# A GRU and a transformer block on one core: queries and keys of six heads instead of four made beside the recurrence, output and feed-forward weights split later

## What is computed

```python
def cell(h, x):                      # 128 steps, one after the other
    gi, gh = x @ W_ih + b_ih, h @ W_hh + b_hh
    r, z = sigmoid(i_r + h_r), sigmoid(i_z + h_z)
    n = tanh(i_n + r * h_n)
    return (1.0 - z) * n + z * h
x = x + gru(x)                       # B, T, D = 16, 128, 256
x1 = ln(x) * (1 + scale1) + shift1   # scale, shift, gate from the condition
q, k, v = x1 @ qkv_w + qkv_b         # H = 16 heads of DH = 128
a = softmax(q @ k.T * DH ** -0.5) @ v
x2 = x + gate1 * (a @ out_w + out_b)
y = gelu((ln(x2) * (1 + scale2) + shift2) @ ffn_w1 + ffn_b1) @ ffn_w2 + ffn_b2
out = x + x2 + gate2 * y
```

## Time and profile before

| | before |
|---|---|
| median of 3 runs (lowest to highest) | 746.58 us (746.04 to 747.35) |
| the profiled execution's own time | 746.35 us |
| its span, first to last instruction | 744.5 us |
| TensorE busy | 711.3 us (96%) |
| VectorE busy | 580.8 us (78%) |
| ScalarE busy | 484.9 us (65%) |
| GpSimd busy | 104.4 us (14%) |
| chain that ended last | TensorE 83%, VectorE 6%, ScalarE 4%, DMA 3%, issue 2% |

### The profile page before, as it was taken

The page is one execution under the profiler, slowest core; times in us unless marked ns, Lnnn a source line. Parts: engine busy times, 40 slices in busy tenths (PEclk is TensorE's granted clock), DMA queues, the critical chain, the costliest instruction groups (busy, mean ns, idle before and its releaser), DMA issues.

```text
span 744.5 us, 25735 instructions
## 1 busy us (share of the span) xinstructions
PE 711.3 (96%) x10644; PEld 525.3 (71%) x10644; DVE 580.8 (78%) x1625; ACT 484.9 (65%) x1665; POOL 104.4 (14%) x134
## 2 busy tenths in 40 slices
PE   6789999999999989999999999999999999999997
PEld 5688888888888767767667677676666767644555
DVE  5778888888888877777788888788887888834643
ACT  4455666556555666767787777776778776675453
POOL 0232222322322200000000101010110101000040
PEclk9999999999999999999999999999999999999999
DMA  6311121111211012222322222222232233300001
GB/s 237 100 48 46 47 83 51 46 45 46 88 38 40 3 30 43 44 37 49 46 44 44 43 45 44 43 44 49 40 50 43 45 52 37 47 19 29 29 6 52
DMA packets 77869, 36.74 MB, mean 49 GB/s; under 512 B 70540, under 2 KB 73784, under 8 KB 77752
## 3 DMA queue, kind: packets, MB, share of 16 engines
q1 hardware_dynamic: 77175, 33.52, 20.4%
q10 hardware_dynamic: 576, 1.57, 0.6%
HBM read 16.20 MB, written 2.10 MB: 25 GB/s over the span
## 4 chain that ended last, share of the span: by engine, by line
PE 83%; DVE 6%; ACT 4%; DMA 3%; issue 2%; SPq 1%; POOL 0%; DVEq 0%; POOLq 0%
PE bank L429 21%; PE bank L431 20%; PE bank L430 20%; PE bank L536 12%; PE bank L544 5%; DVE h_hi L1211 3%; DMA pT_lo<-p_lo 3%; PE bank L449 2%; ACT zg L937 2%; DVE nu L1205 1%; SPq L308 1%; PE bank L436 1%; DMA x<-in_x 1%; PE bank L458 0%; PE bank L478 0%
## 5 line engine op out<-in xcount | busy, mean ns | idle before, releaser
L431 PE MATMUL bank<-y_lo,w_hi 128*128 128x512 f16 (+2 forms) x496 | 139.8, 300 | 0.0
L429 PE MATMUL bank<-y_hi,w_hi 128*128 128x512 f16 (+2 forms) x496 | 139.7, 300 | 0.1
L430 PE MATMUL bank<-y_hi,w_lo 128*128 128x512 f16 (+2 forms) x496 | 139.8, 300 | 0.0
L536 PE MATMUL bank<-h_hi,whh_hi 128*128 128x16 f16 x1536 | 111.1, 177 | 17.6 <-DVE h_hi L1211 15.2
L536 PEld LDWEIGHTS bank<-h_hi,whh_hi 128*128 128x128 f16 x1536 | 88.8, 96 | 36.7 <-DVE h_hi L1211 34.1
L536 PE MATMUL bank<-h_hi,whh_lo 128*128 128x16 f16 x1536 | 109.5, 176 | 0.4 <-issue 0.4
L997 ACT ACTIVATE prob<-bank,nmx 128x128 f32<-128x128 f32 x256 | 90.4, 366 | 29.8 <-DVE nmx L1286 29.8
L536 PEld LDWEIGHTS bank<-h_hi,whh_lo 128*128 128x128 f16 x1536 | 89.4, 96 | 0.6 <-issue 0.5
L429 PE MATMUL bank<-w_hi,y_hi 128*128 128x128 f16 x512 | 89.1, 219 | 0.5 <-DVE v_lo L1290 0.5
L431 PE MATMUL bank<-w_lo,y_hi 128*128 128x128 f16 x512 | 89.1, 219 | 0.0
L430 PE MATMUL bank<-w_hi,y_lo 128*128 128x128 f16 x512 | 89.1, 219 | 0.0
(11 more groups left out here) (156 smaller groups left out, 2132.9 us busy)
## 6 DMA issues: line engine op xcount, KB each, us to landing
stage<-in_weights SPq DMA_DIRECT2D x16, 640.0 KB, 4.1
x<-in_x SPq DMA_DIRECT2D x16, 128.0 KB, 4.0
out<-xr SPq DMA_DIRECT2D x3, 512.0 KB, 3.1
xr<-in_ada_r SPq DMA_DIRECT2D x1, 1024.0 KB, 7.4
pT_hi<-p_hi SPq DMA_TRANSPOSE x64, 2.4
pT_lo<-p_lo SPq DMA_TRANSPOSE x64, 2.5
xr<-in_W_ih ACTq DMA_DIRECT2D x2, 384.0 KB, 3.9
xr<-in_W_hh ACTq DMA_DIRECT2D x2, 384.0 KB, 5.2
```

The source lines that it names most:

```text
L429: mm(ps, w[0], a[0], start=start, stop=False, skip_group_check=True)
L430: mm(ps, w[1], a[0], start=False, stop=False, skip_group_check=True)
L431: return mm(ps, w[0], a[1], start=False, stop=stop, skip_group_check=True)
L536: nc.tensor.matmul(out(m0 + m), half[:, k, (m0 + m) * P:(m0 + m + 1) * P], h_hi[:, k * B:(k + 1) * B, 1], start=False, stop=False, skip_gr ...
```

## The change

1. `AHEAD` is 0, 4, 6, 8, 11, 14. An item is now q or k (one part) of one head for two blocks: 6 matmuls of 256 columns, one high and one low half of 256 columns each. The items run at steps 0, 2, 3, 4, 6, 7 of a block (block 4 also at step 5; block 2 only at step 7), 80 in all, behind the input products of that step. They use all of bank 4. `share` and the tables of the last block are dealt anew.
2. What 80 steps can't hold goes into group 0 of the attention: q and k of heads 11 and 14 for the last four blocks are four items of 6 matmuls of 512 columns ("4q" to "5k"), issued after scores 7, 8, 9 and 10; the item of head 0 for groups 1 to 3 is issued after scores 12.
3. Only the 48 pieces of the q, k and v weights are split in the recurrent stage (256 columns each, blocks 0 to 11). The output weights (8 chunks of 512 columns) are loaded at the end of it, and split by ScalarE and GpSimd in heads 2 to 15, the feed-forward weights (8 chunks) in heads 19 to 56, loaded by Sync between the transposes. They take the space of q and k of finished heads.
4. All eight `modulation` columns are made in block 2, one a step; the load of their weights is issued before the pieces of block 2.

```diff
-PC = WCOLS // (NBL * PB)
+PC = KD * DH
+NPIECE = QCOLS // PC
+NPR = NPIECE // PB
...
-AHEAD = (0, 6, 8, 14)
+AHEAD = (0, 4, 6, 8, 11, 14)
...
-ITEMS = [(e, n, 1, 0, B, 4, 2 * P) for n in range(NBL - 2) for e in range(NA)]
+PART_AT, PART_AT_2, PART_AT_4 = (0, 2, 3, 4, 6, 7), (7,), (0, 2, 3, 4, 5, 6, 7)
+PART_STEPS = [(r, s) for r in range(FIRST_R, NBL) for s in {2: PART_AT_2, 4: PART_AT_4}.get(r, PART_AT)]
+PAIRS = [(e, (part,), 2 * j, 2, 0, B, 4, 0) for j in range(NBL // 2 - 1) for e in range(NA) for part in range(2)]
+ITEMS = PAIRS[:len(PART_STEPS)]
...
+              3: (3, (0, 1), NBL - 2, 2, 0, B, 4, 0), "4q": (4, (0,), NBL - 4, 4, 0, B, 4, 0),
...
+ISSUED = {5: 3, 7: "4q", 8: "4k", 9: "5q", 10: "5k", 12: "rest"}
+LATER = {4: 2, 6: 3, 8: "4q", 9: "4k", 10: "5q", 11: "5k", 13: "rest"}
+OUT_HIGH = {5: 2, 7: 3, 9: 4, 11: 5, 12: 6, 14: 7}
+FF_LOAD = {g * H + i: (g - 1) * 3 + n for g in range(1, NG) for n, i in enumerate((1, 5, 9)) if (g - 1) * 3 + n < FF_CHUNKS}
+FF_HIGH = {d + 2: c for d, c in FF_LOAD.items()}
+FF_LOW = {d + 1: c for d, c in FF_HIGH.items()}
...
+            sp.wait_ge(z_mm, (NBL - 1) * BS + 1)
+            for i in range(OUT_CHUNKS // 2):
+                sp.dma_start(flat_xr2[:, 2 * i * CW:2 * (i + 1) * CW], weights[:, QCOLS + 2 * i * CW:QCOLS + 2 * (i + 1) * CW]
+                             ).then_inc(wo_in[i], 16)
...
             for d in range(HEADS):
                 turn(d)
+                if d in FF_LOAD:
+                    load_ff(FF_LOAD[d])
...
+            def out_low(i):
+
+                pool.wait_ge(wo_h, i + 1)
+                hi, lo = out_chunk(i)
+                gtt(lo, out_stage(i), hi, sub).then_inc(wo_l, 1)
...
+            for d, i in OUT_HIGH.items():
+                behind_max(d + 1)
+                out_low(i)
+            for d in range(H, HEADS + 1):
+                g, i = d // H - 1, d % H
+                if d in FF_LOW:
+                    behind_max(d)
+                    ff_low(FF_LOW[d])
...
-            share = (0, 0, 7, 9, 22, 25, 31, 32, 36)
+            share = (0, 0, 9, 14, 19, 24, 36, 36, 36)
...
-                        if r > 1:
-                            ahead(NA * (r - 2))
                         rows_T(r - 1)
...
+                    if (r, s) in ITEM_AT:
+                        if ITEM_AT[r, s] == 0:
+                            pe.wait_ge(ada_add, ADA - G1 - 1)
+                        ahead(ITEM_AT[r, s])
...
-                if d in (5, 8):
-                    ahead(LAST[2 if d == 5 else 3])
+                if d in ISSUED:
+                    ahead(LAST[ISSUED[d]])
...
-                    if r > 1:
-                        ahead_low(NA * (r - 2) + s // 2, [s % 2])
+                    if (r, s) in ITEM_AT:
+                        ahead_low(ITEM_AT[r, s])
```

More of the change, by code:

```diff
@@ L503, in tall_parts, with ahead @@
                 return mm
-            def ahead(item, parts=(0, 1)):
-                e = ITEMS[item][0]
+            def ahead(item):
+                e, parts = ITEMS[item][0:2]
                 for part in parts:
                     ps, b, t = ahead_place(item, part)
-                    if part == 0:
+                    if part == parts[0]:
                         pe.wait_ge(lb_lo, t.stop // BS)
@@ L591, in _ @@
                         rows_back(r - 1)
-                    if 0 <= r - MOD_FROM < (ADA - G1) // 2 and s == 7:
-                        pe.wait_ge(rest_in, 16)
-                        pe.wait_ge(lb_lo, r)
-                        for i in range(2):
-                            modulation(G1 + 2 * (r - MOD_FROM) + i)
                     if r < NBL - 1:
@@ L613, in _ @@
                         row_modulation(*ROW_TILES[s])
-                    elif r == NBL - 1:
-                        if s == 1:
-                            pe.wait_ge(piece_lo, QKV_PIECES)
-                            pe.wait_ge(lb_lo, NBL - 2)
-                        for i in range(tall_at[s], tall_at[s + 1]):
-                            tall_parts(tall_rest[i % 6:i % 6 + 1], WHOLE[0], i // 6, early)
+            ahead(LAST["old"])
             pe.wait_ge(lb_lo, NBL - 1)
@@ L809, in _ @@
             scores(1)
-            ahead(LAST["rest"])
-            pe.wait_ge(piece_lo, NBL * PB)
+            ahead(LAST[2])
             values(1)
@@ L819, in _ @@
             attend(1)
-            queries(4)
             values(3)
@@ L906, in ahead_high @@
             def ahead_high(item):
-                e = ITEMS[item][0]
+                e, parts = ITEMS[item][0:2]
                 act.wait_ge(qk_mm, item + 1)
-                for part in range(2):
+                for part in parts:
                     ps, b, t = ahead_place(item, part)
```

238 lines of the change are left out of this document (153 added, 85 removed).

## The result

| | us |
|---|---|
| changed kernel, median of 4 runs | 740.43 (738.79 to 741.54) |
| kernel before, median of 4 runs beside it | 746.77 (746.04 to 747.35) |
| ratio | 0.9914 [0.9891, 0.9937] |
| profiled execution, and its span | 741.54, 739.7 |
| last new state starts (258.4 before) | 265.1 |

The kernel is faster by 0.9%, and the median is 0.4 us from the forecast. From the page of the changed kernel: busy shares, two DMA queues, the chain of waits by engine, and the new loads (KB each, us to landing).

The account below looks back on a forecast made before the run. It took the recurrence as bound by a latency, the loop of 1.94 us a step, and the attention by TensorE's issue. Attention -11.4 and recurrence +5.7 gave -5.7 from 746.58, about 740.8 us; range 735 to 746.

Parts of the forecast that it names:

- Products, -15.6: Attention: 96 matmuls of 512 columns go (20.8 us), 24 come in (5.2 us), net -15.6 us of TensorE's issue.
- rival E: Matmuls cost less than their columns, so the 72 net ones give back 9.4 us; ends at 747 us; chance 0.01.
- Bank 4, +0.7: Attention: late q and k items wait for the previous item's low half, 0.5 us after head 8, 0.2 after head 10.
- Transposes, +2.5: Attention: more short heads leave attend waiting longer behind transposes; 8.4 us idle by half is +4, taken +2.5 us, bounds 0 and +8.
- VectorE and ScalarE, +1: Attention: norm steps on mostly short heads and 0.6 us more ScalarE work per chunk cost +1 us, bounds 0 and +3.
- GpSimd and loads, 0: Attention: 16 GpSimd subtractions mostly start behind a head's maximum, and Sync's loads sit behind transposes of finished heads; both cost 0.
- Rival D: Attention: GpSimd's subtractions block the division, at most 1.1 us each, +17.6 if all 16 did: 758 us; chance 0.02.
- Items, +5 in 51 steps: Recurrence: wide items' halves end later, so VectorE's scan starts late; 0.1 us in each of 51 steps, +5 us.
- Rival A: Recurrence takes the wide items for nothing and only step 1 pays, +0.7 us: 736 us; chance 0.2.
- Block 2, -0.75, modulation -0.5: Recurrence: an item at half clock leaves block 2, the clock falling again taken at 0 (bound +2); modulation leaves step 7.
- B: Attention becomes a chain: transposes now and then held, short heads take 5.45 instead of 5.3 us: 744.5 us; chance 0.17.
- C: Recurrence: wide halves push the gates' own instructions, 0.3 us a full step, 15.3 instead of 5: 751 us; chance 0.08.

Follow-up runs that it names:

- late pieces: The changed kernel with keys of the sixth head's last piece and the rest of the last block each made one head later: 740.18 us, ratio 0.9913.
- bank 5: The changed kernel with the items of steps 3 and 6 made in bank 5 in place of bank 4: 736.97 us, ratio 0.9873.
- four edits together: The changed kernel with bank 5 items, seven input products in step 1, 83 unused matmuls in blocks 1 and 2, and late pieces: 740.53 us, ratio 0.992.
- fewer products: The changed kernel with seven input products in step 1, three instead of five in steps 2 to 4, four in steps 6 and 7: 740.34 us, ratio 0.9902.
- seven products: The changed kernel with seven instead of nine input products in step 1, the two moved to steps 6 and 7: 738.88 us, ratio 0.9887.

## Why the prediction was right

The time came out at the forecast, and the split between the stages nearly so: attention -11.8 us (-11.4 forecast), recurrence +6.7 to the last state and +0.3 from there to the first maximum (+5.7 together). The mechanism was right in the large: products taken off a bound TensorE, paid for in part by wide items in the recurrence. That the total came within 0.4 us is also luck. Inside the stages several terms were off and cancelled, and where the instruction packets fall, which no term has, moves other versions by 6 to 7 us.

- *Products, -15.6:* right, 15.5 measured. The page "TensorE: Matmul & The Clock Gate" of the Trainium skill (section "Back-to-back issue gap") gives about 131 ns a product, by which an estimated 9.4 us would have gone. The measured 15.5 us, 0.215 us a product, contradict it: rival E is refuted.
- *Bank 4, +0.7:* the right mechanism, mis-sized. 0.29 us at 320.4 and 0.98 at 335.8, together 1.3. The second is "5k" after head 10, for which 0.2 was put. The run with late pieces removes it, and the time hardly moves.
- *Transposes, +2.5:* failed at the step that took 8.4 us by half for idle time that grows with the short heads. TensorE's gaps behind pT_lo went from 3.0 to 1.6 us. Short heads do leave enough time for the transposes that land in the usual 2.45 us. What decides is whether a packet of instructions makes pT_lo land late, and in which head. With the same attention but for two late pieces, the gaps behind pT_lo were anything from 0.4 us (bank 5) to 10.2 us (four edits together).
- *VectorE and ScalarE, +1:* too small. The gaps behind aT_lo went from none to 3.1 us and those behind xn from none to 0.7. Without the splits those behind aT_lo are 0.7 us, in head 5 of group 0, and the attention is 1.2 us shorter. The two misses, -3.9 and +2.8, cancel: waits of +4.2 were forecast, +3.7 measured.
- *GpSimd and loads, 0:* right for the loads as far as the traces show, wrong for GpSimd. The two subtractions that don't start behind a maximum run into `nmx`, and the first delays aT_lo by 0.82 us, ahead of a gap of TensorE of 1.07 us. That is part of what stands under VectorE above. Rival D had the right mechanism at the wrong instruction and far too large.
- *Items, +5 in 51 steps:* the place was right, the size and the law wrong. Step 0 pays little (+0.21 over blocks 3 to 15), steps 2 to 4 pay 0.04, 0.07 and 0.06 in the blocks 7 to 14, together +2.05 over blocks 3 to 15: 2.3 us instead of 5. The step that failed is "start of ScalarE = filler's length less 0.39" as what sets the step. With fewer products it stayed where it was in steps 3 and 4, and in step 2 it moved and the step did not. In items of consecutive steps it is the one place in bank 4, a loop of 1.99 us, that sets it, which the bank 5 run shows; in step 2 it is VectorE's order. Rival A's reason, that unequal fillers don't matter, was right but for this.
- *Step 1, +1.4:* right, +1.27. The run with seven products takes it back.
- *Block 2, -0.75, modulation -0.5:* the modulation right (step 7: -0.39). Block 2 failed: +2.32 instead of -0.75. The possibility was named, and taken at 0. The fall did not cost "some tenths": it lasted 13.6 us, four steps took 2.6 to 2.9 us, and the block took 3.1 us more than in the trace where the clock stayed up in it (18.73 against 15.61). That is beyond the bound of +2 too.
- *Block 0:* +1.42 in this execution, not forecast. TensorE stood 1.46 us with "issue" as the only reason (19.87 us); in other executions of the same instructions the step took 2.44 instead of 3.59. It is no effect of the change.
- *Stage end, +0.5:* +0.27.

Rival A is refuted by the items' steps, though by only 2.3 us in all. B, C and D did not come: the short heads of groups 1 to 3 took mostly 5.3 us (4.9 to 6.1), no items' step of blocks 7 to 14 paid more than 0.07 on average, no division waited. (By the rivals' own chances faster adds up to 0.80 and slower to 0.10; 0.81 and 0.09 were written.)

One rival stood in no forecast and is untested: that part of the gain is itself a matter of where the packets fall, since the change takes 264 matmuls out. The gaps behind pT_lo fell by 1.4 us, so up to about that much of the 6.3 us may be chance. No run separates it.

## What to carry to other kernels

Look for loops beside the main one: work that is spread one piece a step over a single buffer has a period of its own (here 0.14 + 0.86 + 0.99 us), and when it is longer than the step, it is the step; a second buffer for two of its six pieces in a block cost nothing in the recurrence here. Give a term for waits on DMA that share engines with instruction traffic as a wide range, and before judging an edit that moves the time by less than 1%, shift the instruction stream by some dozens of matmuls and see how much of it stays. And a combination that wins less than its parts is worth an explanation: here it led to the largest single effect of the study.
